# Softmax attention on one core: the weighted sums spread between the scores of each pair of tiles

## The reference

```
q = _qdq(x) @ _qdq(wq).T + bq
kv = cond @ wkv.T + bkv
k, v = jnp.split(kv, 2, axis=-1)
...
attn = jax.nn.softmax(jnp.einsum('bnhd,bmhd->bhnm', q, k) * scale, axis=-1)
o = jnp.einsum('bhnm,bmhd->bnhd', attn, v).reshape(B, N, C)
out = _qdq(o) @ _qdq(wp).T + bp
```

## Time and profile before

| | us |
|---|---|
| median of three runs | 1968.57 |
| profiled execution, its own time | 1969.23 |
| span of the profile | 1967.4 |
| attention loop, first score to the next stage's first matmul | 330.5 to 629.8 |
| TensorE busy in 330.5 to 630.0 | 278.88 of 299.50 |
| VectorE busy there | 176.58 |
| ScalarE busy there | 142.08 |

### The profile page before, as it was taken

One profiled execution on the slowest core, in us unless ns is written; L12 is line 12 of the kernel. 1 busy time (PEld: TensorE's weight loads), 2 busy tenths in 40 slices (PEclk: granted clock), 3 DMA queues, 4 the chain that ended last, 5 costly groups with the idle time before them and its releaser, 6 DMA issues. The chain is left out here.

```text
span 1967.4 us, 25447 instructions
## 1 busy us (share of the span) xinstructions
PE 1866.6 (95%) x9816; PEld 1419.8 (72%) x9816; DVE 1246.6 (63%) x2196; ACT 664.4 (34%) x1054; POOL 225.5 (11%) x192
## 2 busy tenths in 40 slices
PE   7899999899999999989999999999999999999997
PEld 5677887444443589758888888888778775788885
DVE  5423755675762655486787787778662488765665
ACT  3312232345444455433342333333234331221211
POOL 0000100211200000011111211211200001212211
PEclk9999998999999999999999999999999999999999
DMA  5101321233322100032313313214211110111001
GB/s 215 44 0 55 102 70 45 58 73 71 95 49 83 47 1 1 25 113 74 101 53 112 103 38 132 84 38 132 75 45 65 64 43 0 65 43 43 22 1 43
DMA packets 67191, 124.16 MB, mean 63 GB/s; under 512 B 8576, under 2 KB 27008, under 8 KB 65536
## 3 DMA queue, kind: packets, MB, share of 16 engines
q1 hardware_dynamic: 67072, 122.53, 19.9%
HBM read 88.82 MB, written 14.68 MB: 53 GB/s over the span
## 5 line engine op out<-in xcount | busy, mean ns | idle before, releaser
L784 DVE TENSOR_REDUCE b_nm<-ps 128x1 f32<-128x1024 f32 x128 | 153.2, 1219 | 86.6 <-PE ps L772 86.4
L1265 ACT ACTIVATE b_pr<-ps 128x512 f32<-128x512 f32 x256 | 133.4, 603 | 129.4 <-PE ps L1179 129.2
L229 PE MATMUL ps<-d_x_high,d_w_high 128*128 128x512 f32 x384 | 154.3, 402 | 1.7 <-issue 1.7
L231 PE MATMUL ps<-d_x_high,d_w_low 128*128 128x512 f32 x384 | 149.8, 390 | 0.0
L230 PE MATMUL ps<-d_x_low,d_w_high 128*128 128x512 f32 x384 | 149.7, 390 | 0.0
L1191 PE MATMUL ps<-b_pr,b_VS 128*64 128x512 f32 x512 | 127.0, 618 | 0.0
L1179 PE MATMUL ps<-b_qS,b_kS 98*128 98x512 f32 x256 | 92.7, 445 | 6.9 <-ACT b_pr L1265 3.5
L2168 POOL TENSOR_TENSOR d_sqsum<-d_sqsum,d_sq 128x512 f32<-128x512 f32 x32 | 45.4, 1422 | 468.3 <-ACT d_sq L2079 468.1
L1179 PEld LDWEIGHTS ps<-b_qS,b_kS 98*128 98x128 f32 x256 | 43.4, 190 | 75.8 <-issue 49.3
L772 PE MATMUL ps<-b_kS,b_qS 96*128 96x512 f32 x256 | 82.9, 409 | 5.9 <-DVE b_nm L784 4.5
L229 PEld LDWEIGHTS ps<-d_x_high,d_w_high 128*128 128x128 f32 x384 | 72.2, 188 | 17.3 <-issue 2.1
(11 more groups left out here) (429 smaller groups left out, 4826.7 us busy)
## 6 DMA issues: line engine op xcount, KB each, us to landing
b_kS<-b_k_parts SPq DMA_DIRECT2D x96, 128.0 KB, 2.3
f_rows<-d_fw SPq DMA_DIRECT2D x24, 512.0 KB, 3.3
f_w<-f_rows SPq DMA_DIRECT2D x12, 1024.0 KB, 4.8
b_qS<-b_q_parts SPq DMA_DIRECT2D x96, 64.0 KB, 2.0
a_convT<-in_convT SPq DMA_DIRECT2D x4, 1024.0 KB, 12.9
d_w<-in_d_wq SPq DMA_DIRECT2D x16, 256.0 KB, 3.8
d_w<-in_d_wk SPq DMA_DIRECT2D x16, 256.0 KB, 2.8
d_w<-in_d_wg SPq DMA_DIRECT2D x16, 256.0 KB, 3.9
```

What stands on the lines that cost most here:

```text
L229: nc.tensor.matmul(out, lhsT[0], rhs[0], start=start, stop=False)
L231: return nc.tensor.matmul(out, lhsT[1], rhs[0], start=False, stop=stop)
L784: nc.vector.tensor_reduce(nm[:, g % 2, u:u + 1], c.ps[:, banks:banks + 2, :], AX.XY, ALU.max, negate=True).then_inc(job_read, 1)
L1265: nc.scalar.activation(pr[:, n % RING, :], c.ps[:, 4 + n % BANKS, :], ACT.Exp).then_inc(exp_done, 1)
```

## The change

The two weighted sums of a turn stood together behind all its scores and jobs. Now each half of the turn has one of them, behind its two scores and ahead of its jobs.

```diff
                     if ss < NSS:
                         scores(4 * ss + 2 * half)
                         scores(4 * ss + 2 * half + 1)
+                    if ss >= 1:
+                        weigh(4 * (ss - 1) + 2 * half)
                     for j in JOBS_AT[2 * ss + half]:
                         job(j)
-                if ss >= 1:
-                    weigh(4 * (ss - 1))
-                    weigh(4 * (ss - 1) + 2)
```

## The result

The change takes 1979.04 us (median of 6 runs, 1974.41 to 1984.14) against 1970.05 us for the kernel before in the same series (1968.54 to 1976.11). The ratio is 1.0045, 95% interval 1.0031 to 1.0059: slower by about 9 us, where +4.5 was forecast; 1979.04 lies inside the range of 1966 to 1981, near its upper end. The profiled execution took 1977.72 us for a span of 1974.9; against the profile of before that is 7.5 us of span.

The account below looks back on a forecast made before the run. The prediction took TensorE's own sequence to bound the stage: −1.7 us for the first group and +6.2 for the rest make +4.5, against the runs' median 1973.1 us (+0.23%), range 1966 to 1981 us.

Parts of the forecast that it names:

- The price of a block: On TensorE, entering, running and leaving a weighing block costs 0.35 us beyond its records; 63 added blocks make 22.1 us.
- The change's turn: Sign in the middle groups: the repeated turn of scores, weighing and maxima takes 4.3 us in place of 3.96.
- the entry from scores: Sign on TensorE: two scores to the weighing behind them take 0.56 to 0.58 us start to start.
- the rival of the dear entry: Slower rival: entering weighing from scores costs 0.10 us more per block, +17.1 in all, 1985.7 us; chance 0.13.
- The faster rival: Weight loads of short blocks hide behind running matmuls, so added switches cost nothing: −17.6, 1951.6 us; chance 0.06.
- The waits given back: From 379.5 us on, waits of transposes, maxima and scores that the new order removes: 14.7 us.
- the new wait for the row transfers: In the last group, four slots too short to cover the way from L779 to the next scores: 1.0 us new.
- first group: −1.7: From 330.5 to 379.5 us: +4.2 for work put ahead of the transpose, −7.4 waits removed, +1.5 wait that stays.
- The leg behind L779: In the first group, from the maxima's transpose to the first score needing them: stays 7.67 us.
- The clock: Case of a clock that falls longer before the second group or again elsewhere: 2 to 5 us more; chance 0.12.
- +6.2 for all the others: From 379.5 us on: 56 added blocks +19.6, waits given back −14.7, new waits +1.3.

Follow-up runs that it names:

- e2: e1 with its block split, two weighing matmuls before the fourth score and two behind it (126 blocks); 1987.01 us, ratio 1.0081 to the kernel before.
- e1: Kernel before with the block of four weighing matmuls moved between the third and fourth score of a turn (64 blocks); 1976.89 us, ratio 1.0023.
- e9: e7 with its block cut in two, two weighing matmuls on each side of the second score (127 blocks); 2003.34 us, ratio 1.0163 to the kernel before.
- e7: Kernel before with the block of four weighing matmuls moved between the first and second score of a turn (64 blocks); 1986.34 us, ratio 1.0073.
- e3: The change with each slot's weighing behind the slot's jobs instead of ahead of them (126 blocks); 1977.59 us, ratio 1.0034 to the kernel before.
- e4: The change with group 2's first eight maxima moved from slots 10 to 17 into slots 14 to 17; 1969.17 us, ratio 0.9991 to the kernel before.
- e10: Kernel before with the changed order only in turns 0 to 7 and from 52 on, plus e4's move of maxima; 1967.48 us, ratio 0.9987.
- e6: Kernel before with only e4's move of group 2's first eight maxima (63 blocks); 1972.52 us, ratio 1.0002.
- e8: e7 with e4's move of group 2's first eight maxima added (64 blocks); 1977.18 us, ratio 1.0023 to the kernel before.
- e11: e10 with two weighing matmuls ahead of slot 11's maximum and two before the maxima's transpose, groups 1 to 5; 1958.76 us, ratio 0.9935 to the kernel before.
- e12: e11 with weighing also split around the jobs in six turns holding a pair's transpose alone (93 blocks); 1959.54 us, ratio 0.9937 to the kernel before.

## Why the prediction was right, and where it was not

**The price of a block (0.35 us) was right.** The change's turn is 4.30 us where the prediction said 4.3, the entry from scores 0.56 where it said 0.56 to 0.58, and e2 against e1 (0.35) and e9 against e7 (0.34) give it by itself. This also settles the rival of the dear entry: the 0.43 us of the earlier trace rows was the reload after a stalled score, not the switch. The faster rival (load hidden in short blocks) fell with the same rows.

**The waits given back were right from the second group on.** No L1167 and no L772 waits for VectorE after 380, no score waits for an exponential at the end, L779 still waits 0.9 each. Groups 2 and 3 grew by 2.0 us each, for eight blocks (2.8) less 0.8. Groups 6 and 7 became shorter: from the first score of group 7 to the end of the loop 29.6 us now, 30.6 before, with the new wait for the row transfers in it at 0.72 us (forecast 1.0):

```profile
607.17 1.08 PE L1191 MATMUL ps<-b_pr,b_VS 128*64 128x512 f32 x4
608.96 0.73 PE L1179 MATMUL ps<-b_qS,b_kS 98*128 98x512 f32 x2 [0.72 <-DMA b_qS<-b_nm_parts]
```

**The step that failed is "first group: −1.7".** It measured +1.8 in the profile. The working let TensorE arrive earlier at everything in the group, but looked at operands only for group 1. Group 2's operands come by a chain of their own over GpSimd and the queue, which ended at 358.0 before, 1.7 us ahead of TensorE, and at 359.1 after. With TensorE earlier by 4.4 us, up to 3.4 of it by a clock that rose sooner, it met that chain and waited 3.9 us; the step put this wait at nothing. Its size belongs to this one execution: in e3, where the clock rose as late as before, the wait is 0.73 and the first group is 2.6 us shorter than before. The leg behind L779 took 8.0 us in place of the 7.67 that the step kept.

**The clock** was a case of its own (2 to 5 us, 0.12), and a part of it came. Group 1 ran at 0.89 after, at 0.95 before, which is some 2.7 us of its 3.7 (half of what 41.3 and 37.6 us had at 1.2 GHz, an estimate). Over executions: the six of the change have a mean granted clock of 0.9833 and a mean span of 1977.0 us, 23 of the kernel before, in the series of e1, 0.9847 and 1969.4. That is 3 us more not granted; at 0.8 to 1 us of span for each, 2 to 3 of the 7.6 us between them are clock, by this estimate over two series. What is left, about 5 us, is close to the +4.5 of the order alone. The profiled execution had the highest clock of the six (0.986) and long waits, so its shares need not be those of the others. Whether the longer wait before group 1 brings the clock down stays open: before that group TensorE stood idle for 3.5 us in the change (10.3 us at half the clock behind it), 1.6 before (3.5), 1.4 in e4 (none) and 1.4 in e10 (6.8).

In sum the shares of the 7.5 us between the two profiles: first group +1.8, group 1 +3.7, groups 2 to 7 +3.6, and −1.6 outside the loop, where nothing was changed. The forecast had −1.7 for the first group and +6.2 for all the others, which measured +7.3, with the 2.7 us of clock in them.

## What to carry to other kernels

Count how often a sequence switches between two kinds of matmuls, here full width in float32r and half width in float32: each switch there and back costs 0.35 us of TensorE in this kernel, so such work is best done in blocks, and a block is to be cut only where it hides a wait longer than that. Before moving a block, list what stands on both sides of it and who used the time: three places for the same block (behind the jobs, inside the second half, inside the first half) differed by 6 to 14 us in their medians, each time with a wait in the trace that the old place had hidden. And when waits are removed at the start of a stage, ask which transfer with a fixed time is met next. A single profile can mislead about where time went: compare when the clock rose and fell in both before giving a difference to the order.

## What the runs showed that I had not expected

- The place of the blocks can outweigh their number: e7 with 64 blocks (1.0073) is slower than the change with 126 (1.0045).
- With the late maxima in the old order (e6), in e8 and in e10, groups 4 and 5 had stretches at half the clock; in e6 and e10 each of these groups is 1.3 to 1.6 us longer than before. The stretches begin within 1.5 us of the 1.3 us waits of the maxima's transpose. e4, e11 and e12, which also have the late maxima, had no such stretch, and no wait of that transpose over 0.9 us there; the kernel before had the waits and no stretch. What decides it stays open.
- Splitting the weighing in the order of e1 cost only 10 us, in the order of e7 17: the price of a block is seen in full only where no wait is hiding in it.
